# Value tile ahead of the key's sum, seven written-out expert loops with bounds in registers, a spread routing chain, and the share fused into the expert's output

## What is computed

```python
def xattn(x, context, Wq, Wk, Wv):            # 32 heads of 16
    q, (k, v) = heads(x @ Wq.T), heads_interleaved(concat(context @ Wk.T, context @ Wv.T))
    q, k = rmsnorm(q), rmsnorm(k)
    attn = softmax(einsum('bhnd,bhmd->bhnm', q, k) * 16 ** -0.5)
    return einsum('bhnm,bhmd->bhnd', attn, v)

def ffn(x, ...):                              # 7 routed experts, the top 2 of a token, 1 shared
    gate = xt @ Wr + br
    _, ids = top_k(gate + gate_bias, 2)
    probs = softmax(gate kept at ids, -inf elsewhere)
    u = xt @ Wup[e] + bup[e]
    g = silu(u @ Wgate[e] + bgate[e]) * u
    out = sum over e of probs[:, e] * (g @ Wdown[e] + bdown[e])
    return out + the same three products with the shared expert's weights

x = x + xattn(layernorm(x), ctx, ...)
x = x + ffn(layernorm(x), ...)
```

## Time and profile before

| | us |
|---|---|
| median of 3 runs (982.33 to 983.61) | 982.45 |
| the profiled execution | 984.33 |
| its span, first to last instruction | 982.6 |
| PE, DVE, ACT, POOL busy | 952.8, 707.1, 497.6, 203.3 |
| idle time ahead of a product, sum's largest: `sum_k` (L671) for VectorE's release of `tr` | 5.9 in 5 waits |
| TensorE's mean granted clock, as a share of 2.4 GHz | 0.992 |

### The profile page before, as it was taken

The page is one execution under the profiler, slowest core; times in us unless marked ns, Lnnn a source line. Parts: engine busy times, 40 slices in busy tenths (PEclk is TensorE's granted clock), DMA queues, the critical chain, the costliest instruction groups (busy, mean ns, idle before and its releaser), DMA issues.

```text
span 982.6 us, 18038 instructions
## 1 busy us (share of the span) xinstructions
PE 952.8 (97%) x6720; PEld 685.5 (70%) x6721; DVE 707.1 (72%) x1460; ACT 497.6 (51%) x619; POOL 203.3 (21%) x209
## 2 busy tenths in 40 slices
PE   7999999999999999999999999999999999999995
PEld 6633443454443553345989998999989999999995
DVE  6798667876778757885968985855857576858653
ACT  4588568866787568887333222422424243424221
POOL 1011000311012200321100000333233333233331
PEclk9999999999999999999999999999999999999998
DMA  9400100100201020223411242543644536635523
GB/s 331 163 1 22 65 1 1 44 33 12 86 2 43 38 71 1 83 79 102 189 66 44 75 156 97 159 109 53 177 83 103 143 76 190 183 66 152 120 52 41
DMA packets 32217, 86.28 MB, mean 88 GB/s; under 512 B 7712, under 2 KB 7712, under 8 KB 28064
## 3 DMA queue, kind: packets, MB, share of 16 engines
q1 hardware_dynamic: 21632, 59.65, 16.9%
q0 software_dynamic: 10528, 25.87, 13.1%
HBM read 61.83 MB, written 23.67 MB: 87 GB/s over the span
## 4 chain that ended last, share of the span: by engine, by line
PE 85%; DVE 10%; issue 2%; DMA 1%; ACT 1%; DVEq 0%; POOLq 0%; SPq 0%; POOL 0%; ACTq 0%
PE z_ps L875 16%; PE y_ps L875 15%; PE u_ps L875 15%; PE o_ps L611 10%; PE scores L595 7%; PE bank_b L632 5%; PE bank_a L648 4%; PE bank_b L618 2%; PE xt_ps L887 2%; PE bank_a L618 2%; PE tr L671 2%; PE tr L666 1%; PE tr L677 1%; DMA ctx_raw<-ctx_t 1%; DVE k_lo L1390 1%
## 5 line engine op out<-in xcount | busy, mean ns | idle before, releaser
L1144 ACT ACTIVATE probs<-scores 128x2048 f32<-128x2048 f32 x128 | 240.7, 1880 | 77.6 <-PE scores L595 74.6
L875 PE MATMUL z_ps<-u_hi,w_sb 128*128 128x256 f32 x896 | 167.9, 285 | 1.4 <-DVE u_lo L1819 1.4
L875 PE MATMUL u_ps<-x_hi,w_sb 128*128 128x256 f32 x864 | 159.4, 283 | 3.0 <-issue 3.0
L1174 ACT ACTIVATE u_hi<-u_ps,b_ug 128x256 fp32r<-128x256 f32 x108 | 45.4, 471 | 199.9 <-PE u_ps L875 199.9
L875 PEld LDWEIGHTS z_ps<-u_hi,w_sb 128*128 128x128 f32 x896 | 140.6, 190 | 2.7 <-DVE u_lo L1819 1.8
L875 PE MATMUL y_ps<-w_sb,g_hi 128*128 128x512 f32 x448 | 139.5, 392 | 0.0
L875 PEld LDWEIGHTS u_ps<-x_hi,w_sb 128*128 128x128 f32 x864 | 135.5, 190 | 5.5 <-issue 4.5
L611 PE MATMUL o_ps<-probs,v_sb 128*17 128x512 f32 x1024 | 136.4, 605 | 0.0
L875 PE MATMUL z_ps<-u_lo,w_sb 128*128 128x256 f32 x448 | 126.3, 282 | 0.0
L875 PE MATMUL u_ps<-x_lo,w_sb 128*128 128x256 f32 x432 | 121.9, 282 | 0.0
L1186 ACT ACTIVATE s_sb<-z_ps,b_ug 128x256 f32<-128x256 f32 x112 | 47.1, 472 | 105.7 <-PE z_ps L875 105.7
(11 more groups left out here) (246 smaller groups left out, 1579.6 us busy)
## 6 DMA issues: line engine op xcount, KB each, us to landing
w_raw<-w_all SPq DMA_DIRECT2D x27, 1024.0 KB, 6.9
ctx_raw<-ctx_t SPq DMA_DIRECT2D x4, 1024.0 KB, 7.3
out<-x_sb SPq DMA_DIRECT2D x16, 256.0 KB, 2.0
x_sb<-x SPq DMA_DIRECT2D x1, 3072.0 KB, 16.2
xn<-x_t SPq DMA_DIRECT2D x12, 256.0 KB, 4.4
xn_dram<-xn SPq DMA_DIRECT2D x12, 256.0 KB, 2.1
xt_dram<-xt SPq DMA_DIRECT2D x6, 512.0 KB, 3.0
xg<-xt_dram POOLq DMA_DIRECT2D x10, 256.0 KB, 3.2
```

What stands on the lines that cost most here:

```text
L875: ins = nc.tensor.matmul(out_ps, stat[a], mov[b], start=(first and a + b == 0), stop=(last and a == 1), skip_group_check=True)
L1144: nc.scalar.activation(probs[:, t % 2], scores[:], ACT.Exp).then_inc(p_ready, 1)
L1174: last = nc.scalar.activation(u_hi[:, c, :], u_ps[:, b, a, :], ACT.Identity, bias=b_ug[:, par, 0, c:c + 1])
```

## The change

1. **Attention.** In units 2, 6 and 10 (`more and g == 2`) step 2 had `sum_k` ahead of `weighed` and `v_even` behind it. Now `sum_k` comes behind `v_even`, and VectorE's `v_out` comes ahead of `sums_k`.
2. **Shared expert's splits.** VectorE's splits of the third weight move from units 12 and 13 to units 13 and 14, and one of the high parts goes to ScalarE, ahead of the exponential of unit 13, step 7.
3. **Routing.** `hot_rows(0)` moves from `during_u` of tile 4 to its `during_y`; `hot_cols(0)` from there to `during_u` of tile 5; `hot_cols(1)` from `during_y` of tile 5 to `during_u` of tile 6. Expert 1's splits move: the first from tile 3 to tile 2, the second to the end of tile 6, the third from tile 6 to tile 7. SyncE loads expert 2's weights one by one behind tiles 2, 6 and 7 (stores 5, 13, 15).
4. **Loops.** TensorE, ScalarE and VectorE run `experts`: seven loops one behind the other, with the expert's number known when the code is built. Seven bounds are loaded ahead: by TensorE within y of tiles 5 and 6, by ScalarE and VectorE in `during_y` of tile 7. SyncE and GpSimd keep `routed`.
5. **Share.** In a routed tile VectorE first writes `bd` × share into `y_sb` (two instructions, ahead of the wait for y) and then `y_ps` × share + `y_sb` in one instruction for each half, in place of L1847 and L1854.

```diff
+        def experts(engine, start_at, head, tile, first_tile=None):
+            for j in range(1, ER + 1):
+                head(j, j % 2, j // 2)
+                first = start_at[j - 1]
+                if first_tile is not None:
+                    first_tile(j, first + NA, j % 2)
+                    first = first + 1
+                with engine.Fori(first, start_at[j]) as i:
+                    tile(i + NA, j % 2, j)
+
+        def bound(engine, e):
+            return engine.value_load(start_i[0:1, e:e + 1], min_val=0, max_val=MOST)
...
+            def load_weight(j, m):
+                sp.wait_ge(lo_done, j * 6 + 2 * m - 10)
+                sp.dma_start(w_raw[:, m], w_all[j, :, m]).then_inc(raw_loaded[m], 16)
...
-                elif t == 11:
-                    sp.wait_ge(lo_done, 6)
-                    load_weights(2)
+                elif t in (5, 13, 15):
+                    load_weight(2, (5, 13, 15).index(t))
...
-                    if u + 1 < UNITS:
+                    if u + 1 < UNITS and not (more and g == 2):
                         sum_k(u + 1)
...
                 if s == 2 and more and g == 2:
                     v_even(u)
+                    sum_k(u + 1)
...
+                    if c < len(bounds):
+                        start_at.append(bound(pe, bounds[c]))
...
-            routed(pe, head, tile)
+            experts(pe, start_at, lambda j, par, nth: pe.wait_ge(lo_done, j * 6), tile)
...
-            FFN_AHEAD = {(UNITS - 2, 6): (first_weight_high, 0, 0), (UNITS - 2, 7): (first_weight_high, 0, 1),
+            FFN_AHEAD = {(UNITS - 3, 7): (first_weight_high, 2, 3), (UNITS - 2, 6): (first_weight_high, 0, 0), (UNITS - 2, 7): (first_weight_high, 0, 1),
...
-                elif at == (-4, 7):
+                elif at == (-3, 6):
                     first_weight(2, 1)
-                elif at == (-3, 6):
+                elif at == (-2, 2):
                     first_weight(2, 2)
-                elif at == (-3, 7):
-                    first_weight(2, 3)
+                elif at == (-2, 3):
+                    first_weight_low(2, 3)
...
-                    if more and g == 3:
+                    if more and g >= 2:
                         v_out(b + 1, 2 * g - 4)
                     if nxt:
                         sums_k(u + 1)
-                    if more and g == 2:
-                        v_out(b + 1, 2 * g - 4)
...
+                    for h in range(2):
+                        nc.vector.tensor_scalar(y_sb[:, h, :], bd[:, par, :], row_now[:, h, j - 1:j], None, ALU.mult)\
+                          .then_inc(y_biased, 1)
...
-                        share = row_now[:, h, bass.ds(j - 1, 1)] if not isinstance(j, int) else row_now[:, h, j - 1:j]
-                        nc.vector.tensor_scalar(at, at, share, None, ALU.mult).then_inc(y_scaled, 1)
+                        nc.vector.scalar_tensor_tensor(at, y_v[:, h, :], row_now[:, h, j - 1:j], at, ALU.mult,
+                                                       ALU.add).then_inc(y_done, 1)
```

More of the change, by code:

```diff
@@ L912, in table_part, with tile @@
                 last.then_inc(window_ready, 1)
-            def tile(n, par, j=0, behind_up=None, amid_z=None, behind_z=None, windows=0):
+            def tile(n, par, j=0, behind_up=None, amid_z=None, behind_z=None, windows=0, bounds=()):
                 w = w_sb[par]
@@ L973, in _ @@
             tile(4, 0)
-            tile(5, 0, behind_up=lambda: table_part(5, 0), windows=2)
-            tile(6, 0, behind_up=lambda: table_part(6, 1), windows=3)
+            start_at = [0]
+            pe.wait_ge(start_ready, 1)
+            tile(5, 0, behind_up=lambda: table_part(5, 0), windows=2, bounds=range(1, DC + 1))
+            tile(6, 0, behind_up=lambda: table_part(6, 1), windows=3, bounds=range(DC + 1, ER + 1))
             for n in range(7, NA):
                 tile(n, 0)
-            def head(j, par, nth, first):
-                pe.wait_ge(lo_done, j * 6)
-                pe.sem_inc(passed)
-            routed(pe, head, tile)
+            experts(pe, start_at, lambda j, par, nth: pe.wait_ge(lo_done, j * 6), tile)
         @block.scalar
@@ L1201, in _, with bounds, head @@
             tile(3, 0, during_z=choice_exp, during_y=splits(1, 1, [2]))
-            for n in range(4, NA):
+            for n in range(4, NA - 1):
                 tile(n, 0)
-            def head(j, par, nth, first):
+            start_at = [0]
+            def bounds():
+                act.wait_ge(start_ready, 1)
+                for e in range(1, ER + 1):
+                    start_at.append(bound(act, e))
+            tile(NA - 1, 0, during_y=bounds)
+            def head(j, par, nth):
                 act.wait_ge(b_loaded[par], nth * 32 + 32)
@@ L1887, in last_split, with bounds, head @@
                 split(1, 1, 2)
-            tile(6, 0, x_tile=12, during_u=last_split, before_x=lambda: table_out(1))
-            for n in range(7, NA):
-                tile(n, 0, x_tile=2 * n)
-            def head(j, par, nth, first):
+            tile(6, 0, x_tile=12, during_u=lambda: hot_cols(1), before_x=lambda: table_out(1),
+                 during_y=splits(1, 1, [1]))
+            start_at = [0]
+            def bounds():
+                dve.wait_ge(start_ready, 1)
+                for e in range(1, ER + 1):
+                    start_at.append(bound(dve, e))
+            tile(7, 0, x_tile=14, during_u=last_split, during_y=bounds)
+            def head(j, par, nth):
                 dve.wait_ge(b_loaded[par], nth * 32 + 32)
-                dve.sem_inc(passed)
             def first_tile(j, n, par):
-                if isinstance(j, int):
+                if j == ER:
                     tile(n, par, j)
@@ L1906, in first_tile @@
                          during_z=lambda: split(j + 1, 1 - par, 1, [0]), during_y=rest)
-            routed(dve, head, tile, first_tile)
+            experts(dve, start_at, head, tile, first_tile)
 def kernel(**inputs):
```

27 lines of the change are left out of this document (15 added, 12 removed).

## The result

| | before | after |
|---|---|---|
| median of 4 runs, us | 982.88 | 976.07 (975.58 to 977.60) |
| profiled execution, us | 984.33 | 975.58 |
| its span, us | 982.6 | 973.9 |
| mean granted clock | 0.992 | 0.995 |

The ratio of the times is 0.9933, with a 95% interval of 0.9916 to 0.9950: a gain of 6.8 us, where 10.9 were forecast. 976.07 lies 4.6 us above the forecast and just outside its range. The kernel is faster, but a part of the gain went back in a place that the forecast did not look at.

A forecast was written before the change was run, and what follows sets the result against it. TensorE, busy 952.8 of 982.6 us, was taken as the bound. Terms 4.9 + 3.2 − 0.2 + 1.3 + 1.0 − 2.2 + 2.5 + 0 + 0.4 = 10.9 us, so 982.45 − 10.9 = 971.5 us, range 967.5 to 976.0.

The forecast's parts named there:

- Entry into expert 1 gives nothing: Entry into tile 8: VectorE's seven loads delay y; TensorE starts 1.0 us earlier but waits 1.5, net 0.
- The clock behind it: Attention, units 2 and 10: without idle time ahead, no stretch at the lower clock; 2 × 1.6 = 3.2 us gained.
- the three waits of the sum: Units 2, 6, 10: the key's sum behind the value tile no longer waits for `tr`; 4.9 us gained.
- tile 4: Routing: TensorE's wait of 0.88 us for `u_lo` behind `hot_rows` goes; 1.0 us gained.
- tiles 5 and 6: Routing: `hot_cols` between the halves of `u_lo` makes `table_part` wait 1.1 us in each tile; 2.2 us lost.
- the heads: Second and third pair of expert loops: TensorE's waits of "issue" for loading bounds go; 2.5 us gained.
- The share's 0.4: Last tile: the first half is ready for the scatter without the multiply; 0.4 us gained.
- The splits: Shared expert, units 13 and 14: moving VectorE's splits removes two waits of the key's sum; 1.3 us gained.
- (a): Rival: the routing and the entry cost nothing, TensorE keeps 2.2 and 1.0 us more; 968.3 us, chance 0.14.
- (b): Rival: two low-clock stretches remain or come elsewhere, costing 3.2 us; 974.7 us, chance 0.13.
- (c): Rival: attention's wait moves to ScalarE's exponential behind the later sum, losing the 8.1 us; 979.6 us, chance 0.06.
- (d): Rival: each of 13 loop jumps back fetches its body anew, 0 to 4.2 us each; slower, chance 0.05.

The follow-up runs named there:

- the loops alone: The kernel before with part 4 of the change and nothing else; 983.33 us, ratio 1.000.
- the loads spread: The changed kernel with VectorE's seven loads of bounds spread over tiles 4 to 7 instead of all ahead of y of tile 7; 974.92 us, ratio 0.9916.
- the gather cured: The changed kernel with GpSimd waiting for a scatter's landing ahead of the next scatter, not the next gather; 970.97 us, ratio 0.9877.
- the weights later: The changed kernel with SyncE holding an expert's weights back until the gather of the expert's third tile has landed; 971.03 us, ratio 0.9877.

## Why the prediction was wrong, step by step

**The failed step is "Entry into expert 1 gives nothing".** It followed the loads of bounds from VectorE to TensorE, by way of `u_lo`, and there it was not far off: the loads took 4.5 us (597.4 to 601.9) and not 5.3, the wait of z is 0.54 and not 1.5, and so the entry gave 1.0. It did not follow the other way out of VectorE: y of tile 7, which those loads delay, is also what SyncE's last store waits for, behind it GpSimd's whole queue, and behind that TensorE's rows for tile 10. That queue's first gather was issued 6.4 us ahead of expert 3's weights and had landed 1.2 us ahead of them, and the forecast had no row on this distance. The runs showed 5.0 us lost in tile 9: 3.18 of wait with overlap, and a low stretch behind it. That the gather meets the weights is shown by two runs, each of which parts them (970.97 and 971.03). That part 4 brings the wait is shown by the loops alone (1.78). How much of it the seven loads make is not isolated: with the loads spread the wait was the same, and something else held the store back.

**"The clock behind it" was right in its mechanism and wrong in its size.** With the waits gone no low stretch is left in attention. But 3.2 us are what two low stretches cost in the profiled execution. The median execution has about one, by the mean clocks: the gain in the profiled executions is 8.75 us, in the medians 6.8. The prediction noted that the profiled execution took 1.9 us more than the median and then subtracted its whole sum from the median. Of the 1.9 between the two gains, 1.45 are the kernel before (984.33 against 982.88), and 0.5 the kernel after, whose profiled execution is the fastest of its four (975.58 against 976.07).

These two, 5.0 and 1.9, are more than the 4.1 missing, since 1.0 at the entry, 1.0 at the start, 0.6 in units 2, 6 and 10 and 0.3 at the end came on top. The start's 1.0 is luck. With the gather cured, 970.97 us stand beside the 971.5 forecast, but by terms that cancel.

**Right in size**: the three waits of the sum; tile 4; tiles 5 and 6 (two waits of 0.89, 1.06 with overlap, forecast 1.1), confirmed by the run that removes them; the heads, confirmed by the run that brings them back. The share's 0.4 is neither confirmed nor refuted: 0.7 in the two traces, 0.2 and 0.8 when it is undone. **A little off**: the new wait for the exponential in unit 2 was forecast at 0.2 and is 0.54 (TensorE's scores at 101.72), since ScalarE's logarithm started at 99.18, behind a wait of 2.79 for VectorE. The splits gave 0.9 of 1.3, since the transposes of unit 14, "on time by a tenth now", come 0.4 later, 0.17 of it a wait.

**The rivals.** (a) is out for the routing (the waits came) and right for the entry. (b), a low stretch that comes elsewhere, came true in tile 9, 1.6 us, though not behind the waits it named. (c) is out but for one unit. (d) is out: TensorE's list of waits has no line of "issue" left, so none of the 13 jumps back costs it a wait that shows. From 620 to 963 the queue of instruction blocks (q8) brings 6 blocks, as many as there are experts behind the first, and not the 13 of the jumps (which engine's blocks come by q14, 3 in the earlier trace rows, the views don't say):

```profile
q8 instruction: 6, 0.10, 0.1%
```

The rule in the Trainium skill, "Runtime: NRT & Kernel Launch", section "Instruction fetch mechanics", that a branch out of the window waits for a fetch, shows nowhere here as a wait of TensorE.

## What to carry to other kernels

Where work is put into a gap of an engine, follow every reader of what that engine does next, down to the queues that issue transfers, and not only the reader that feeds the bound engine; then write down how far each small transfer lies from the next large one. A transfer of a few rows that feeds the bound engine should not be queued behind a store or scatter it doesn't depend on. And before a term on a disturbance that comes and goes is subtracted from a median, ask how many of them the median execution has.

## What the runs showed of the hardware

**A small gather beside large loads.** Alone it took 3.6 to 4.0 us from issue to landing; beside 3 MB of weights it landed 7.7 us after its second issue (620.16 to about 627.9). The Trainium skill says in "Trainium Kernel Development and Optimization", section "Key Constraints", that DMAs issued from the SP, ACT and POOL queues all run on the same 16 DMA engines and interleave. The trace agrees in that the small transfer of one queue took twice its time beside the large one of another. It made little difference whether the weights began 0.1 or 1.2 us behind the second issue (7.7 and 7.6 us to landing); 3.9 us behind it, the gather had landed. The waits of 1.78, 2.72 and 3.18 us go with how far the second issue stood ahead of the moment at which TensorE wanted the rows: 5.9, 4.8 and 4.7 us.

**A block of instructions delays a store.** The 16 KB block took 1.6 us on one DMA engine, and the store that had eight packets left behind it landed in 3.9 us and not 2.3. The Trainium skill, "Runtime: NRT & Kernel Launch", section "Instruction fetch mechanics", calls the cost of crossing into the next block mostly hidden. No wait of TensorE shows it here, but the store does.

**GpSimd's copy ends with VectorE's split.** The copy of 128 × 2 numbers takes 0.18 us alone and 1.28, 0.80 and 0.84 in three kernels when a split runs, and ends 0.04 us behind the split each time. This agrees with the Trainium skill, "SBUF — State Buffer", section "SBUF: two separate sides": an operation of VectorE with two inputs in SBUF and one of GpSimd that reads SBUF exclude each other for their whole length. No run was made to test it. Where the copy met the end of the first of two splits in a row, it took 0.18 in one kernel (607.87, with the weights later) and 1.28 in another (607.18, the changed kernel); which of the two follows is open.

**The clock.** Waits of 3.18 and 2.72 us in tile 9 were followed by a stretch at the lower level (1.2 GHz) in each profile that has them; those of 1.56 to 1.78 us were in some places and not in others. No run was made on what makes the difference.
